# Another order in the opening of the macaron layer kernel on one core: normalisation before the counts, weights of layer 1 by output tile, the flag ahead of a cast

## What is computed

```python
def ffn(x):
    h = silu(tlin(x, w1_w, w1_s)) * tlin(x, w2_w, w2_s)          # 128 -> 512
    h = gelu(tlin(h, h1_w, h1_s), approximate=False)             # 512 -> 512
    h = gelu(tlin(h, h2_w, h2_s), approximate=False)             # 512 -> 512
    return tlin(h, w3_w, w3_s)                                   # 512 -> 128
def attn(x):                                                     # tanh recurrence over the 512 tokens
    xB = einsum('bsd,dn->sbn', x, B)
    hs = scan(h = tanh(xb_t + h @ A.T))
    return (hs @ C) @ W_out.T + b_out
x = x + 0.5 * ffn(layernorm(x))
x = x + attn(layernorm(x))
x = x + 0.5 * ffn(layernorm(x))
```

## Time and profile before

| | |
|---|---|
| median of 3 runs | 382.91 us (382.40 to 382.96) |
| the profiled execution | 382.39 us, of which the span of the instructions is 380.4 us |
| PE (TensorE) busy | 373.4 us, 98% of the span |
| DVE (VectorE) | 280.2 us, 74% |
| ACT (ScalarE) | 261.0 us, 69% |
| POOL (GpSimd) | 177.6 us, 47% |
| chain that ended last | PE 96%, ACT 2% |

### The profile page before, as it was taken

The page is one execution under the profiler, slowest core; times in us unless marked ns, Lnnn a source line. Parts: engine busy times, 40 slices in busy tenths (PEclk is TensorE's granted clock), DMA queues, the critical chain, the costliest instruction groups (busy, mean ns, idle before and its releaser), DMA issues.

```text
span 380.4 us, 6512 instructions
## 1 busy us (share of the span) xinstructions
PE 373.4 (98%) x1773; PEld 297.2 (78%) x1773; DVE 280.2 (74%) x711; ACT 261.0 (69%) x605; POOL 177.6 (47%) x161
## 2 busy tenths in 40 slices
PE   7999999999999999999999999999999999999995
PEld 6877777878788787878778788888888888887774
DVE  5978988887787977677968876767867677786713
ACT  3889485667758678675684767858576785857653
POOL 2645265575746558342452623535233353533421
PEclk9999999999999999999999999999999999999998
DMA  7920010102001020000001000010100001010001
GB/s 235 434 108 1 28 57 28 57 2 83 3 28 56 2 83 0 28 1 29 28 2 55 3 28 28 2 55 1 55 0 27 28 0 55 0 52 7 2 28 32
DMA packets 7805, 16.64 MB, mean 44 GB/s; under 512 B 1888, under 2 KB 2912, under 8 KB 7520
## 3 DMA queue, kind: packets, MB, share of 16 engines
q1 hardware_dynamic: 6768, 16.01, 11.2%
q10 hardware_dynamic: 1008, 0.29, 0.3%
HBM read 9.99 MB, written 2.12 MB: 32 GB/s over the span
## 4 chain that ended last, share of the span: by engine, by line
PE 96%; ACT 2%; issue 0%; DVE 0%
PE F L288 75%; PE FR L288 8%; PE SC L504 2%; PE FR L316 1%; PE F L541 1%; PE SC L436 1%; PE F L532 1%; PE MI L316 1%; PE MI L296 1%; PE FR L306 1%; PE SC L288 1%; PE F L534 1%; PE SC L451 1%; ACT y_hi L1235 1%; PE MI L458 0%
## 5 line engine op out<-in xcount | busy, mean ns | idle before, releaser
L288 PE MATMUL F<-y_hi,w_hi 128*128 128x512 f32 (+1 forms) x484 | 196.9, 407 | 0.3 <-DVE y_lo L1059 0.2
L288 PE MATMUL F<-y_lo,w_hi 128*128 128x512 f32 (+1 forms) x484 | 188.4, 390 | 0.0
L288 PEld LDWEIGHTS F<-y_hi,w_hi 128*128 128x128 f32 x484 | 91.0, 188 | 24.0 <-issue 6.0
L1232 ACT ACTIVATE y<-F,sc 128x512 f32<-128x512 f32 x111 | 76.0, 685 | 43.1 <-PE F L288 41.9
L288 PEld LDWEIGHTS F<-y_lo,w_hi 128*128 128x128 f32 x484 | 91.2, 188 | 15.3
L853 DVE TENSOR_TENSOR y_lo<-y,y_hi 128x512 fp32r<-128x512 f32 x79 | 66.3, 839 | 39.9 <-ACT y_hi L1235 39.9
L1506 POOL TENSOR_TENSOR y_lo<-y,y_hi 128x512 fp32r<-128x512 f32 x48 | 66.6, 1394 | 58.7 <-DVE y_hi L840 48.1
L1512 POOL TENSOR_TENSOR y_lo<-y,y_hi 128x512 fp32r<-128x512 f32 x48 | 62.5, 1309 | 35.1 <-ACT y_hi L1235 35.1
L1235 ACT ACTIVATE y_hi<-F,sc 128x512 fp32r<-128x512 f32 x111 | 75.9, 684 | 0.0
L1251 ACT ACTIVATE h<-SC 128x32 fp32r<-128x32 f32 x96 | 18.8, 195 | 49.3 <-PE SC L451 48.3
L288 PE MATMUL F<-xn_hi,w_hi 128*128 128x512 f32 x118 | 49.4, 419 | 0.0
(11 more groups left out here) (177 smaller groups left out, 438.8 us busy)
## 6 DMA issues: line engine op xcount, KB each, us to landing
w_raw<-mr_row SPq DMA_DIRECT2D x5, 512.0 KB, 3.4
x_all<-in_xT SPq DMA_DIRECT2D x1, 2048.0 KB, 16.2
x_all<-x1c SPq DMA_DIRECT2D x8, 256.0 KB, 2.3
x_all<-lnin SPq DMA_DIRECT2D x8, 256.0 KB, 2.2
out<-outb SPq DMA_DIRECT2D x7, 256.0 KB, 2.0
x_all<-in_xtok SPq DMA_DIRECT2D x1, 1536.0 KB, 12.1
w_raw<-in_h1T SPq DMA_DIRECT2D x2, 512.0 KB, 7.7
w_raw<-in_h2T SPq DMA_DIRECT2D x2, 512.0 KB, 9.0
```

The source lines that it names most:

```text
L288: mm = nc.tensor.matmul(out, wtile(w, layer, k, m), y, start=first and i == 0, stop=last and i == len(pairs) - 1)
L1232: nc.scalar.activation(y23[:, m, :], bankt[:, :], ACT.Gelu, scale=s)
```

## The change

It changes the opening in six ways.

1. Chunk 0 is normalised before the scales are prepared and before the first count.
2. w1T and w2T become one input w12T, in which the tiles of 128 columns of both weights alternate by output tile m. It is loaded in a piece of 256 columns (tile 0) and one of 768. ACT casts the first before xn_hi, and the second in two parts behind it, so that w_hi_ready counts one more from there on. POOL splits 256, 256 and 512 columns, and PE waits for these before tiles 0, 1 and 2.
3. The count over h1T's first half moves from before DVE's first gate to between the gates of tiles 1 and 2.
4. DVE writes `general` before it casts w3, not behind it.
5. PE multiplies 13 zeros, not 19.
6. a_raw, b_rep and mask are loaded by SP, behind all its other loads.

The diff:

```diff
@@ -46,7 +46,7 @@
 EPS = 1e-5
-WARM = 19
+WARM = 13
 TURNED = 3
@@ -58,7 +58,7 @@
 
-def build(nc, xT, xtok, w1T, w2T, h1T, h2T, w3T, scales, Ablk, Brep, CTrep, WoutT, ident_d, mask_d, outT):
+def build(nc, xT, xtok, w12T, h1T, h2T, w3T, scales, Ablk, Brep, CTrep, WoutT, ident_d, mask_d, outT):
     with ExitStack() as ctx:
@@ -74,7 +74,7 @@
         HALF = KT * HID // 2
-        PIECES = [(0, HID), (HID, HID)] + [(WOFF[2] + i * HALF, HALF) for i in range(4)] + [(WOFF[4], KT * P)]
+        PIECES = [(0, 2 * P), (2 * P, 2 * HID - 2 * P)] + [(WOFF[2] + i * HALF, HALF) for i in range(4)] + [(WOFF[4], KT * P)]
         COUNTED = 5
@@ -246,6 +246,9 @@
 
+            if layer < 2:
+                off = (2 * m + layer) * P
+                return w[:, off:off + P]
             width = P if layer == 4 else HID
@@ -507,7 +510,7 @@
                 w = [[wtile(part, layer, 0, 0) for part in (w_hi, w_lo)] for layer in (0, 1)]
-                pe.wait_ge(w_hi_ready, 2)
+                pe.wait_ge(w_hi_ready, 1)
                 pe.wait_ge(xn_hi_r, 1)
@@ -560,7 +563,7 @@
                 layer1(1, 1, gen)
-                pe.wait_ge(w_hi_ready, len(PIECES) - 1)
+                pe.wait_ge(w_hi_ready, len(PIECES))
                 pe.wait_ge(w3_hi_ready, 1)
@@ -736,8 +739,9 @@
             first_layer1()
+            pe.wait_ge(w_lo1_ready, 2)
             layer1(0, 1, True)
-            pe.wait_ge(w_lo1_ready, 2)
+            pe.wait_ge(w_lo1_ready, 3)
             layer1(0, 2, True)
@@ -748,6 +752,7 @@
             first_layer2(1)
+            pe.wait_ge(w_hi_ready, 5)
             first_layer2(2, range(KT - 1))
@@ -1087,6 +1092,10 @@
             i.then_inc(var["f"], 1)
+            dve.wait_ge(rstd["f"], 1)
+            for q in range(QT):
+                nc.vector.tensor_scalar(xnt_f[:, q * P:(q + 1) * P], cols(xt_all, 0)[:, q * P:(q + 1) * P], mv_f[:, q, 0:1],
+                                        rs_f[:, q:q + 1], ALU.subtract, ALU.mult).then_inc(normed_first if q < QT - 1 else normed["f"], 1)
             dve.wait_ge(ld_sc, 16)
@@ -1094,20 +1103,16 @@
             count(0)
-            dve.wait_ge(rstd["f"], 1)
-            for q in range(QT):
-                nc.vector.tensor_scalar(xnt_f[:, q * P:(q + 1) * P], cols(xt_all, 0)[:, q * P:(q + 1) * P], mv_f[:, q, 0:1],
-                                        rs_f[:, q:q + 1], ALU.subtract, ALU.mult).then_inc(normed_first if q < QT - 1 else normed["f"], 1)
-            count(1)
             dve.wait_ge(xn_hi_r, 1)
...
             mean_negated(1)
-            count(2)
+            count(1)
             layer1(0, 0)
             layer1(0, 1)
+            count(2)
             layer1(0, 2)
@@ -1116,10 +1121,10 @@
             nc.vector.reduce_sum(ne_sum[:, :], ne_cnt[:, :], axis=mybir.AxisListType.X).then_inc(ne_ready, 1)
+            dve.wait_ge(gen_mm, 1)
+            nc.vector.tensor_scalar(general[:, :], SC[0:1, 0:1], 0.0, None, ALU.is_gt).then_inc(gen_ready, 1)
             off, width = PIECES[-1]
             nc.vector.tensor_copy(w_hi[:, off:off + width], w_raw[:, off:off + width]).then_inc(w3_hi_ready, 1)
-            dve.wait_ge(gen_mm, 1)
-            nc.vector.tensor_scalar(general[:, :], SC[0:1, 0:1], 0.0, None, ALU.is_gt).then_inc(gen_ready, 1)
             first_stats(2)
@@ -1394,26 +1399,25 @@
 
-            def hi_part(i):
-                off, width = PIECES[i]
+            def hi_part(i, cut=slice(None)):
                 act.wait_ge(ld_w[i], 16)
+                lo, hi, _ = cut.indices(PIECES[i][1])
+                off, width = PIECES[i][0] + lo, hi - lo
                 nc.scalar.copy(w_hi[:, off:off + width], w_raw[:, off:off + width]).then_inc(w_hi_ready, 1)
...
             act.dma_start(wout[:, :], WoutT).then_inc(ld_cw, 16)
-            act.dma_start(a_raw[:, :], Ablk).then_inc(ld_scan, 16)
-            act.dma_start(b_rep[:, :], Brep).then_inc(ld_scan, 16)
-            act.dma_start(mask[:, :], mask_d).then_inc(ld_scan, 16)
             act.wait_ge(set_up, 1)
...
             hi_part(0)
-            hi_part(1)
             act.wait_ge(feat_first, 1)
...
             nc.scalar.copy(xn_hi[:, N // 2:N], F[1][:, N // 2:N]).then_inc(xn_hi_r, 1)
+            hi_part(1, slice(0, 2 * P))
+            hi_part(1, slice(2 * P, None))
             hi_part(2)
@@ -1567,20 +1571,17 @@
             pool.wait_ge(normed["f"], 1)
-            pool.wait_ge(ld_w[0], 16)
-            pool.wait_ge(ld_w[1], 16)
-            pool.wait_ge(w_hi_ready, 2)
-            for half in range(2):
-                part = [w[:, 0:WOFF[2]].rearrange("p (l n) -> p l n", l=2)[:, :, half * HID // 2:(half + 1) * HID // 2]
-                        for w in (w_lo, w_raw, w_hi)]
-                pool.tensor_tensor(part[0], part[1], part[2].bitcast(F32), ALU.subtract).then_inc(w_lo1_ready, 1)
+            for i, (lo, hi) in enumerate(((0, 2 * P), (2 * P, 4 * P), (4 * P, 2 * HID))):
+                pool.wait_ge(w_hi_ready, i + 1)
+                pool.tensor_tensor(w_lo[:, lo:hi], w_raw[:, lo:hi], w_hi[:, lo:hi].bitcast(F32),
+                                   ALU.subtract).then_inc(w_lo1_ready, 1)
             inverse_std("f", 1, mv_f, ve_f, rs_f)
...
             with pool.If(is_general != 0):
-                pool.wait_ge(w_hi_ready, len(PIECES) - 1)
+                pool.wait_ge(w_hi_ready, len(PIECES))
                 pool.wait_ge(w3_hi_ready, 1)
@@ -1623,14 +1624,16 @@
                 sp.dma_start(xt_all[:, i * N // 2:(i + 1) * N // 2], xtok[:, i * N // 2:(i + 1) * N // 2]).then_inc(ld_x0[i], 16)
-            for i, (w, lo, hi) in enumerate(((w1T, 0, HID), (w2T, 0, HID), (h1T, 0, HALF), (h1T, HALF, 2 * HALF),
-                                             (h2T, 0, HALF), (h2T, HALF, 2 * HALF), (w3T, 0, KT * P))):
+            for i, (w, lo) in enumerate(((w12T, 0), (w12T, 2 * P), (h1T, 0), (h1T, HALF), (h2T, 0), (h2T, HALF), (w3T, 0))):
                 if i == 2:
...
                 off, width = PIECES[i]
-                sp.dma_start(w_raw[:, off:off + width], w[:, lo:hi]).then_inc(ld_w[i], 16)
+                sp.dma_start(w_raw[:, off:off + width], w[:, lo:lo + width]).then_inc(ld_w[i], 16)
             sp.dma_start(xt_all[:, 2 * N:], xtok[:, 2 * N:]).then_inc(ld_x, 16)
             sp.dma_start(x_all[:, :], xT).then_inc(ld_xall, 16)
+            sp.dma_start(a_raw[:, :], Ablk).then_inc(ld_scan, 16)
+            sp.dma_start(b_rep[:, :], Brep).then_inc(ld_scan, 16)
+            sp.dma_start(mask[:, :], mask_d).then_inc(ld_scan, 16)
 
@@ -1700,7 +1703,9 @@
                                 x[TURNED:].reshape(SPREAD, P, QT, P).transpose(1, 0, 2, 3).reshape(P, -1)], axis=1),
-        "w1T": tiles(v["ffn_w1_w"]), "w2T": tiles(v["ffn_w2_w"]), "h1T": tiles(v["ffn_h1_w"]),
+        "w12T": np.ascontiguousarray(np.stack([tiles(v[n]).reshape(P, KT, P) for n in ("ffn_w1_w", "ffn_w2_w")],
+                                              axis=2)).reshape(P, -1),
+        "h1T": tiles(v["ffn_h1_w"]),
         "h2T": tiles(v["ffn_h2_w"]), "w3T": tiles(v["ffn_w3_w"]),
```

## The result

The changed kernel takes **383.01 us** in the median of 22 runs (382.28 to 384.0), the kernel before 382.16 in 22 runs on the same chip: a ratio of 1.002 with a 95% interval of 1.0012 to 1.0028. That is 0.85 us slower, where 0.32 us faster was forecast. The value lies in the range given, but that is luck: the range stood on 382.91, the median of 3 runs of before, and that kernel's median in 22 runs is 0.75 lower. Measured from there the change goes the other way.

What follows compares the result with a forecast made beforehand. PE was taken as the bound, busy from 44 us on, so only its opening counted: -0.07 us at layer 2's third output plus 0.39 from the flag gives 0.32 us earlier, forecast 382.5 us, range 381.8 to 383.4.

Steps and rivals of the forecast that it cites:

- Zero matmuls, 19 to 13: Opening, PE: the 13th zero is done by 6.65 us and holds back nothing that is ready before 6.6.
- First matmul at 8.40: Layer 1, PE: earlier normalisation and fewer zeros start its first matmul 0.68 us earlier; bounds 0.40 and 0.80.
- h1T's cast at 10.0, s = 0.45: Opening, ACT: s is how much earlier h1T's first half lands and is cast (10.43 before); 0.45 us, bounds 0 and 0.9.
- g = s - 0.52: PE at layer 2's third output, 17.33 us before: g is its time gained; s = 0.45 makes it 0.07 us later.
- The stall on y1_r 3: Layer 2's third output near 17.4 us: a new PE wait for DVE's third product y of layer 1, using up 0.68 us.
- The flag, 0.39: DVE writes `general` before casting w3, so PE's matmul L559 starts at 23.91, not 24.30: 0.39 us gained.
- The rival in which DVE takes the gain back: DVE's cast, statistics and normalisation use up the flag's gain: about 0 in all, 382.9 us; chance 0.12.
- Three DMAs moved: nothing: ACT's shorter queue and SP's longer one gain or cost nothing; only h1T's earlier landing counts.
- The clock: Rival: PE's clock is low for layer 1's first eight matmuls, in all 0.8 us slower, 383.7 us; chance 0.13.
- All early: Rival: h1T lands 0.9 us earlier and DVE keeps up, g = 0.38, 0.77 us gained, 382.1 or less; chance 0.13.
- Slower: Outcome: the kernel is slower by over 0.2%, above 383.68 us; chance 0.11.

Runs made afterwards that it cites:

- e5: The changed kernel with six more zero matmuls in PE's untaken branch (13 run, program as long as with 19): 381.92 us, 1.74 outside the span.
- e9: The changed kernel with three more zero matmuls in PE's untaken branch (13 run, program as long as with 16): 384.35 us, 4.15 outside the span.
- e7: The kernel before with 13 zero matmuls in place of 19 and nothing else: 383.11 us, 2.86 outside the span.
- e4: The changed kernel with 19 zero matmuls in place of 13, all run: 382.58 us, 1.73 outside the span.
- e2: The changed kernel with the loads of a_raw, b_rep and mask back on ACT's queue: 383.05 us, 2.88 outside the span.
- e8: The changed kernel with 16 zero matmuls in place of 13, all run: 384.37 us, 4.16 outside the span.
- e12: The changed kernel with six unrun zeros and the count of h1T's first half cut into 512 columns ahead of tile 2's gate and 512 behind: 381.42 us.
- e1: The kernel before with only the loads of a_raw, b_rep and mask moved to the end of SP's queue: 382.31 us, 1.68 outside the span.
- e3: The kernel before with only the flag `general` written ahead of the cast of w3: 382.10 us, 2.00 outside the span.
- e6: The kernel before with six more zero matmuls in PE's untaken branch (19 run, 25 in the program): 382.10 us, 1.98 outside the span.
- e10: The changed kernel with six unrun zeros in PE's untaken branch and the flag behind the cast of w3 again: 382.38 us, 1.77 outside the span.

## Why the prediction was wrong

- **The step that failed** is the one that carries the sum over to the time: "The profiled execution took 382.39 us, so 382.07 by its own time". It took what lies outside the span, 1.99 us, as a constant. It is 2.79 in the change, and e5 and e9 show that the length of PE's program does this with the same work executed; e7 has the loss with 13 zeros and nothing else. The chain itself was sized well enough: e5, the change with six zeros more in its code, is 0.52 us faster in the means (0.3 to 1.2 by its interval), where 0.32 was forecast.
- **The starting point.** 382.91, the median of three runs, was 0.75 above the median of 22. The forecast of 382.5 missed by 0.5; from 382.16 it would have been 381.84, and the miss 1.17.
- **Zero matmuls, 19 to 13.** They were priced by when they end, and that part held in direction: the span of the change is 0.54 below e4's, between groups. That six matmuls fewer, with their weight loads, also move all of the code behind them was not asked. No view of the span shows it, but the difference of time and span stood in the table of before.
- **First matmul at 8.40.** It came at 8.14. In that execution xnt_f started at 6.03 and not 6.24, and the rest follows it.
- **h1T's cast at 10.0, s = 0.45.** In the profiled run it starts at 9.12, outside the bounds given for a right forecast (9.7 to 10.3). th then waits for PE's sum, the upper bound that the text had set at 0.9: it comes 0.92 earlier. But s is no constant. In nine profiles of kernels with the new opening (the change, e2, e4, e5, e8 to e12) that cast starts between 9.05 and 10.74, mean 9.94; in five with the old one (before, e1, e3, e6, e7) between 10.05 and 10.45, mean 10.31. The mean of s is 0.37. One trace of each kernel had put the cast 1.31 earlier.
- **g = s - 0.52.** With s = 0.92 it gives 0.40; PE's matmul moved from 17.33 to 16.96, 0.37. The stall on y1_r 3 was right, and the 0.52 for this profile; in e5, with th at 11.40 against 11.38, the matmul comes 0.35 later (17.68), so there the step cost 0.33.
- **The flag, 0.39.** `general` stands 0.47 behind ne_sum in place of 0.84 (21.99 to 22.83), the cast fell from 0.85 to 0.41 us, and the statistics behind it still start 0.88 behind ne_sum (0.92 in e10). The Trainium skill, "SBUF — State Buffer", section "Who interferes with whom", has the exclusive lock by which the forecast read the 0.85. The traces agree to some 0.1 us: in the five with the flag behind, the cast ends 0.28 or 0.29 behind POOL's y_lo; in the nine with it ahead, the cast starts in the last 0.12 of y_lo and takes 0.40 or 0.41. The rival in which DVE takes the gain back is out by the distances under e10.
- **Three DMAs moved: nothing** for what follows, and 0.45 for h1T. Right in time for the first (e1), though the span grows by 0.3 and the part outside shrinks by as much. For the second the reason was wrong: e1's cast of h1T is only 0.10 earlier, and e2's, with the three DMAs on ACT's queue, is at 9.88, no later than the mean 9.95 of the eight profiles of the new opening with them on SP. Where the mean of 0.37 comes from, if it isn't scatter, stays open.
- **The clock.** PE waits 0.60 us ahead of 8.14, with only four transposes since the zeros. Layer 1's matmuls then start 0.22 to 0.24 us apart (9.48, 9.72, 9.94, 10.18, 10.41), the 2.4 GHz level. The rival is out.
- **All early** was right for the profiled run's PE chain (0.74 earlier, 0.77 worked out), but over the runs the chain is worth about 0.5 (e5).
- **Slower** had 0.11, all of it from the clock. What came stood among no rivals.

Not settled: why 13 zeros cost 0.9 to 1.1 us outside the span. With 16 a late block of instructions goes with the loss; with 13 the trace has the same packets there as with 19 (the last one 1.5 us behind the span in the change and in e5). If all that lies outside lies behind the span, the execution ends 0.8 to 1.1 us after the start of that packet in the three kernels with 13 zeros (the change, e2, e7), and 0.05 to 0.3 after it in the eleven others. What fills the 0.8 to 1.1 is not in the trace.

## What to carry to other kernels

- Read time less span beside the span, for every run of both kernels. If it moved, an argument over engines doesn't explain the whole result. Pad the program with instructions in an untaken branch until its length is that of the kernel before, and compare again; a page's count of packets ends with the span, so look behind it too.
- An edit that changes the number of instructions is two edits: what they do, and where all the code behind them comes to lie.
- A pass that has slack ahead of a deadline can be cut and dealt out between the urgent ones. e12 did that with one count, and with the code at a good length came out below both kernels: 381.42 us, 0.22% to 0.48% below before.

## What the runs showed of the hardware

- With the same work executed, three matmuls that are never run (each with its weight load) added 1.36 us outside the span (e9 against the change, in means), and six took 1.05 us away (e5). The last packet of queue q14 moved with the first (3.6 us behind the span in e8, 4.0 in e9, 1.5 in the change). That it carries PE's code is argued from this, not shown. The Trainium skill, "Runtime: NRT & Kernel Launch", section "Instruction fetch mechanics", says that the sequencers refill ahead in blocks, mostly hidden, and that a taken branch to code outside the blocks held must wait for a fetch. At the program's end PE does jump over the code for inexact weights. e8 and e9, with their late packet, agree with the rule; the kernels with 13 zeros neither show it nor speak against it.
- The moment at which PE goes from 1.2 to 2.4 GHz differs between executions of nearly the same opening. In 6 to 7 and 7 to 8 us the kernel before had 6 and 7 matmuls under way, e4 4 and 6, with as much work ahead of them (3 and 4 in the two us before, in both). With 19 zeros a late rise holds up the transposes: 8.43 in e4, 7.88 before. With 13 it costs next to nothing: in the changed kernel the zeros take 5.62 us, 0.43 apart almost to the end, in e9 4.57. With xnt_f at 6.03 in both, the transposes start at 6.93 and 6.52, but layer 1 at 8.14 and 8.08. This, and the landing of h1T, is why one profile of each kernel was a poor witness for a few tenths.

The zeros of the changed kernel in PE's timeline, and the stretches of e4 (PE busy, its matmuls, the granted clock, which reads 1.00 through it all, DMA share, GB/s):

```profile
1.47 5.62 PE L507 MATMUL SC<-y_lo 128*128 128x512 f32 x13 [1.47 <-DVE y_lo L1079]
```

```profile
4.00:5.00 1.00, 1.00 (x3) 1.00 0.82 250
5.00:6.00 1.00, 1.00 (x4) 1.00 0.97 260
6.00:7.00 1.00, 1.00 (x4) 1.00 0.96 349
7.00:8.00 1.00, 1.00 (x6) 1.00 0.95 288
```
